# The embedding stage of a four-stage transformer kernel, cut into pipelined rounds, with x1 finished on GpSimd and transposed from its own buffer

## What is computed

```python
# layer 0: adapter with a selected expert, residual, layer norm
hidden = gelu(x @ down_W.T + down_b)
hidden = hidden @ Wsel.T + bsel + domain_emb[idx]
x = hidden @ up_W.T + up_b + x
x = (x - mu) * rsqrt(var + eps) * ln_gamma + ln_beta
# layer 1: adaptive layer norm, projections
x = _ln(x) * (1.0 + scale) + shift          # "x1" of the kernel
q, k, v = x @ Wq + bq, x @ Wk + bk, x @ Wv + bv
# ... attention with a bias of 2 x 16 x 2048 x 2048 and a mask, Wo, feed forward, rotation (layer 2)
# layer 3: U_o, V_o = gram_schmidt(U), gram_schmidt(V), 32 columns of 512 rows each
# basis = U_o @ V_o.T ; the rest of the steering layer
```

## Time and profile before

| | us |
|---|---|
| median of 3 runs | 3924.99 (3924.74 to 3928.07) |
| the profiled execution, its time | 3929.97 |
| its span, first to last instruction | 3927.6 |
| granted PE clock, mean over the span | 0.966 of full |
| PE, DVE, ACT, POOL busy | 3701.7, 2385.5, 2139.4, 2190.1 |

### The profile page before, as it was taken

How to read it: one execution, slowest core, us unless ns; L and a number is a source line. 1 busy time by engine, 2 the same in 40 slices (tenths; PEclk the granted TensorE clock), 3 DMA queues, 4 the chain that set the end, 5 groups by cost and what they waited for, 6 DMA issues and landing times. The chain is left out here.

```text
span 3927.6 us, 80609 instructions
## 1 busy us (share of the span) xinstructions
PE 3701.7 (94%) x32225; PEld 2528.7 (64%) x32225; DVE 2385.5 (61%) x4512; ACT 2139.4 (54%) x2970; POOL 2190.1 (56%) x787
## 2 busy tenths in 40 slices
PE   4888897999999999999999999998799999999997
PEld 2444444888888888888888888887344444444443
DVE  5675673888888888888888888886212111211102
ACT  1222122899998999989999889997111111111110
POOL 2332232999898989989999799996211111111100
PEclk8999898999999999999999999999899999999995
DMA  3334336999999999999999999996300000000005
GB/s 135 114 129 171 129 118 250 359 319 325 321 335 362 325 328 325 328 353 346 323 325 322 358 333 319 327 321 233 149 11 22 33 33 11 22 33 12 11 1 191
DMA packets 209772, 830.94 MB, mean 212 GB/s; under 512 B 23650, under 2 KB 57570, under 8 KB 134148
## 3 DMA queue, kind: packets, MB, share of 16 engines
q1 hardware_dynamic: 205060, 817.53, 60.0%
q10 hardware_dynamic: 4352, 8.39, 0.6%
HBM read 733.04 MB, written 92.80 MB: 210 GB/s over the span
## 5 line engine op out<-in xcount | busy, mean ns | idle before, releaser
L909 POOL TENSOR_TENSOR at_tiles<-at_tiles,at_negmask 128x1792 f32<-128x1792 f32 x512 | 1838.1, 3632 | 241.4 <-DMA at_tiles<-in_bias 204.3
L999 ACT ACTIVATE at_tiles<-at_tiles,at_rmin 128x2048 f32<-128x2048 f32 x512 | 1025.3, 2002 | 78.5 <-DVE at_rmin L1046 78.3
L945 PE MATMUL at_ps_p<-consts,at_tiles 128*128 128x128 f32 x8192 | 1025.6, 272 | 0.1
L945 PEld LDWEIGHTS at_ps_p<-consts,at_tiles 128*128 128x128 f32 x8192 | 931.3, 142 | 36.8 <-ACT at_prob_t L1007 0.6
L1007 ACT ACTIVATE at_prob_t<-at_ps_p 128x512 f32<-128x512 f32 x1536 | 830.2, 596 | 145.4 <-PE at_ps_p L945 145.2
L1046 DVE CUSTOM_DVE_ANT_0 at_tiles<-at_ps_s,at_tiles 128x1024 f32<-128x1024 f32 x512 | 624.7, 1220 | 158.2 <-PE at_ps_s L926 117.5
L926 PE MATMUL at_ps_s<-at_k_stack,at_q_stack 128*128 128x512 f32 x2048 | 680.4, 433 | 37.5 <-DMA at_q_stack<-q_lo 16.7
L1046 DVE CUSTOM_DVE_ANT_0 at_tiles<-at_ps_s,at_tiles,at_rmin 128x1024 f32<-128x1024 f32 x512 | 657.6, 1284 | 18.3
L962 PE MATMUL at_ps_c<-at_prob_t,at_v 128*32 128x128 f32 x16384 | 500.9, 274 | 3.3 <-DMA at_v<-v 1.5
L962 PEld LDWEIGHTS at_ps_c<-at_prob_t,at_v 128*32 128x32 f32 x16384 | 431.7, 110 | 47.0 <-issue 44.6
L1240 PE MATMUL ff_ps_m<-ff_norm_t,ff_w 128*128 128x512 f32 x1024 | 442.2, 592 | 0.8 <-ACT ff_feats L1336 0.8
(11 more groups left out here) (170 smaller groups left out, 2989.0 us busy)
## 6 DMA issues: line engine op xcount, KB each, us to landing
at_tiles<-in_bias SPq DMA_DIRECT2D x512, 1024.0 KB, 9.9
at_k_stack<-k_hi SPq DMA_DIRECT2D x128, 256.0 KB, 7.1
at_k_stack<-k_lo SPq DMA_DIRECT2D x128, 256.0 KB, 9.0
negm<-em_mask_out SPq DMA_DIRECT2D x8, 2048.0 KB, 9.9
at_q_stack<-q_hi SPq DMA_DIRECT2D x128, 128.0 KB, 7.8
at_q_stack<-q_lo SPq DMA_DIRECT2D x128, 128.0 KB, 8.7
at_negmask<-negm SPq DMA_DIRECT2D x32, 512.0 KB, 14.7
at_v<-v SPq DMA_DIRECT2D x64, 256.0 KB, 11.2
```

Of the source, the lines that this page charges most:

```text
L909: pool.tensor_tensor(tiles[:, s, 0:PCOLS], tiles[:, s, 0:PCOLS], negm[:, s, 0:PCOLS], ALU.add).then_inc(s_pool, 1)
L945: last = pe.transpose(ps_p[k][:, y * P:(y + 1) * P], tiles[:, s, t * P:(t + 1) * P], ident)
L999: act.activation(tiles[:, s, :], tiles[:, s, :], ACT.Exp, bias=rmin[:, s, 1:2], scale=-1.0, accum_out=rsum[:, s:s + 1]).then_inc(s_exp, 1)
```

## The change

`embed_stage` is written anew as a pipeline with finer steps; the computation is the same. There are nine rounds r again, each with the front of tile r and the back of tile p = r − 1, but now blocks of the back stand between the steps of the front on PE, and splits between them on DVE.

- PSUM: two banks `ps_t` for transposes, three `ps_q` for the 12 blocks in turn, two `ps_u` for the up product, one `ps_d` for down, expert and the Gram-Schmidt products.
- x1 has a buffer of its own, `x1`, and `x1_t` is double. The x1 transposes of tile r come at the end of round r, two chunks ahead of block 11 and two behind it.
- The first norm is two DVE operations with two tensor inputs: (res − mean) × gamma, then × rstd + beta; POOL's beta is gone. The second norm is applied by ACT (`unit_rows`: res × rstd − mean × rstd), and POOL then multiplies the whole tile, 128x2048, by the scale into `x1` and adds the shift in a second operation of that size.
- A Gram-Schmidt step multiplies on DVE the columns by the current one (264 elements), adds the four chunks up with a `tensor_reduce` to 66 columns, and PE adds over partitions with one matmul against ones. The four steps of a round belong to round r, so they run in rounds 0 to 7; the small products of the end (`gs_end`) are spread over round 8.
- The mask leaves in four pieces of 128x2048 per round through two buffers.

The core of the diff (PE's, ACT's, POOL's and DVE's new order and the new helpers):

```diff
+            def gs_dots(n, k):
+
+                i = STEPS * n + k
+                if k == 0:
+                    pe.wait_ge(s_hid2, n + 1)
+                pe.wait_ge(s_gsr, i + 1)
+                pe.matmul(ps_d[:, 0:2 * (RANK + 1)], ones[:], gs_part[:].rearrange("p m r -> p (m r)"),
+                          start=True, stop=True).then_inc(s_dot, 1)
...
+            x_columns(0, range(DC))
+            for r in range(NT + 1):
+                p, front, back = r - 1, r < NT, r >= 1
+                if front:
+                    down_project(r)
+                if back:
+                    project(p, 0)
+                if front:
+                    expert(r)
+                if back:
+                    project(p, 1)
+                if front:
+                    gs_dots(r, 0)
+                    up_project(r, (0, 1))
+                else:
+                    gs_end(0)
+                    gs_end(1)
+                if back:
+                    project(p, 2)
...
+                    gs_end(4)
+                if back:
+                    project(p, 7)
+                if front:
+                    gs_dots(r, 2)
+                if back:
+                    project(p, 8)
+                if r + 1 < NT:
+                    x_columns(r + 1, (0, 1))
+                if back:
+                    project(p, 9)
+                if r + 1 < NT:
+                    x_columns(r + 1, (2, 3))
+                if front:
+                    gs_dots(r, 3)
+                if back:
+                    project(p, 10)
+                if front:
+                    x1_columns(r, (0, 1))
+                if back:
+                    project(p, 11)
+                if front:
+                    x1_columns(r, (2, 3))
...
+            def unit_rows(n):
+
+                act.wait_ge(s_nmr, n + 1)
+                for j in range(TJ):
+                    act.activation(res[:, j, :], res[:, j, :], ACT.Identity, bias=nmr[:, j:j + 1],
+                                   scale=rstd[:, 1, j:j + 1]).then_inc(s_u, 1)
...
+            def root(n, half):
+                link = Chain(pool, s_plink, 4 + 2 * n + half)
+                pool.wait_ge(s_mv, 2 * n + half + 1)
+                link(pool.tensor_tensor(rstd[:, half, :], mv[:, half, :, 1], eps[:], ALU.add))
+                pool.tensor_tensor(rstd[:, half, :], rstd[:, half, :], minus_half[:], ALU.pow).then_inc(s_rs, 1)
+
+            add_up_bias(0)
+            for r in range(NT):
+                b = batch_of(r)
+                gs_norms(r, 0)
+                root(r, 0)
+                root(r, 1)
+                gs_norms(r, 1)
+                if r + 1 < NT:
+                    add_up_bias(r + 1)
+                gs_norms(r, 2)
+                pool.wait_ge(s_u, 4 * r + 4)
+                after(pool, s_x1_st, 16 * r)
+                if r >= 1:
+                    pool.wait_ge(s_tr, chunk_x1(r - 1, DC - 1) + 1)
+                pool.tensor_tensor(x1[:], res[:], net.ada_scale[:, b, :].unsqueeze(1).broadcast_to([P, TJ, D]),
+                                   ALU.mult).then_inc(s_x1m, 1)
+                gs_norms(r, 3)
+                pool.wait_ge(s_x1m, r + 1)
+                pool.tensor_tensor(x1[:], x1[:], net.ada_shift[:, b, :].unsqueeze(1).broadcast_to([P, TJ, D]),
+                                   ALU.add).then_inc(s_x1, 1)
...
+            def gs_products(src, step):
+                step(v.tensor_tensor(gs_prod[:], src[:], src[:, :, :, 0:1].broadcast_to([P, 2, DC, RANK + 1]), ALU.mult))
+                v.tensor_reduce(gs_part[:], gs_prod[:].rearrange("p m c r -> p m r c"), AX.X, ALU.add).then_inc(s_gsr, 1)
...
+            def gs_project(n, k):
+                i = STEPS * n + k
+                src, to = gs[i % 2], gs[(i + 1) % 2]
+                step = Chain(dve, s_gs, i * 6 + 3)
+                dve.wait_ge(s_nrm, i + 1)
+                step(v.reciprocal(gs_norm[:, 2:4], gs_norm[:, 2:4]))
+                over = gs_norm[:, 2:4].unsqueeze(2)
+                v.tensor_tensor(gs_coef[:], dots[:, :, 1:RANK + 1], over.broadcast_to([P, 2, RANK]),
+                                ALU.mult).then_inc(s_gst, 1)
+                step(v.tensor_tensor(gs_col[:], src[:, :, :, 0], over.broadcast_to([P, 2, DC]), ALU.mult))
+                dve.wait_ge(s_gst, i + 1)
+                step(v.tensor_copy(gsq[:, :, :, i:i + 1], gs_col[:].unsqueeze(3)))
+                step(v.tensor_tensor(gs_proj[:], gs_col[:].unsqueeze(3).broadcast_to([P, 2, DC, RANK]),
+                                     gs_coef[:].unsqueeze(2).broadcast_to([P, 2, DC, RANK]), ALU.mult))
+                step(v.tensor_tensor(to[:, :, :, 0:RANK], src[:, :, :, 1:RANK + 1], gs_proj[:], ALU.subtract))
+                gs_products(to, step)
...
+            def centred(n, j):
+                if j == 0:
+                    dve.wait_ge(s_mv, 2 * n + 1)
+                v.scalar_tensor_tensor(res[:, j, :], res[:, j, :], mv[:, 0, j, 0:1], gamma[:], ALU.subtract,
+                                       ALU.mult).then_inc(s_cen, 1)
+
+            def affine(n, j):
+                if j == 0:
+                    dve.wait_ge(s_rs, 2 * n + 1)
+                dve.wait_ge(s_cen, 4 * n + j + 1)
+                v.scalar_tensor_tensor(res[:, j, :], res[:, j, :], rstd[:, 0, j:j + 1], beta[:], ALU.mult,
+                                       ALU.add).then_inc(s_x0, 1)
+
+            def minus_mean(n):
+                dve.wait_ge(s_rs, 2 * n + 2)
+                v.scalar_tensor_tensor(nmr[:], mv[:, 1, :, 0], -1.0, rstd[:, 1, :], ALU.mult, ALU.mult).then_inc(s_nmr, 1)
...
+                    split(p, 3)
+                if front:
+                    centred(r, 2)
+                    affine(r, 0)
+                    centred(r, 3)
+                    affine(r, 1)
+                    row_stats(r, 1, 0)
+                    affine(r, 2)
+                    row_stats(r, 1, 1)
+                    affine(r, 3)
+                    row_stats(r, 1, 2)
+                    moments(r, 1, row_stats(r, 1, 3))
+                if back:
+                    split(p, 4)
+                if front:
+                    gs_squares(r, 1)
...
+                if front:
+                    minus_mean(r)
+                if back:
+                    split(p, 5)
+                if front:
+                    gs_project(r, 1)
...
+                if back:
+                    split(p, 6)
+                if front:
+                    gs_squares(r, 2)
...
+                if back:
+                    split(p, 7)
+                if front:
+                    gs_project(r, 2)
+                if back:
+                    take_v(p, 0)
+                    take_v(p, 1)
+                if front:
+                    gs_squares(r, 3)
+                if back:
+                    take_v(p, 2)
+                if front:
+                    gs_project(r, 3)
+                if back:
+                    take_v(p, 3)
...
```

557 lines of the change are left out of this document (272 added, 285 removed).

## The result

The changed kernel takes 3869.05 us (median of 4 runs, 3866.31 to 3871.07) against 3926.53 us (3924.74 to 3930.59, 4 runs) for the kernel before on the same chip: 57.5 us less, ratio 0.9852, 95% interval 0.9835 to 0.9869. The prediction was 3871 us in a range of 3832 to 3896.

The account below looks back on a forecast made before the run. PE was taken as busiest, losing time to store waits and the low clock behind them. 101 + 6 × 65.6 + 59.7 + 44 = 598.3 us against 648.87, with 3.5 less behind it, gave 3871 us, range 3832 to 3896.

Parts of the forecast that it names:

- The chain of a round: Steady round followed step by step from the down product through PE, DVE, POOL and ScalarE: 65.6 us.
- The low clock behind the first wait: Block 8, after PE's 6.2 us wait for step 1's products, takes 5.4 instead of 3.4 us; at most 2.0 us loss.
- The lower bound: Steady round if the low clock behind the two PE waits costs nothing: 62.5 us.
- First round: Serial chain of the first tile: down product of round 1 at 101 us against 91.55 today, a loss of 9.5 us.
- The last front round: Round without up bias and x transposes: x1 at 52.9, end at 59.7 us.
- the last round: Round with 12 blocks and the final small products: 44 us.
- pause: Between the embedding stage and attention, waiting for transfers to land: 3.5 us less, bounds 0 and 6.
- 4 × 1.5 = 6 us per round: Gram-Schmidt steps on PE: one 66-column matmul replaces the 16-pass weight loads, a step falling from about 1.7 to 0.2 us.
- Rival A: DVE isn't shut out for whole POOL operations: a round of 61 us, 3839 us in all; chance 0.14.
- Rival B: PE at its floor, waits at both places vanish: 55 us a round, median basis 3798 us; chance 0.04.
- Rival C: Clock stays at 1.2 GHz from first wait to round's end: round about 79 us, 3970 us in all; chance 0.06.
- D: No change: something unseen adds 6 us to a round and the first round loses more, about 3920 us; chance 0.04.

Follow-up runs that it names:

- run 3: Changed kernel with six extra unused matmuls on TensorE ahead of the third small product of rounds 1 to 7: 3868.03 us, ratio 0.9851.
- Runs 6 to 9: On the kernel before: em_res twice, 3873.63 us; one small product per step, 3932.95; both edits, 3885.19; both with each small product issued eight times, 3884.85.
- run 5: Kernel of run 4 with shift straight behind scale, fourth small product inside block 11, and VectorE splitting blocks 6 and 7 later: 3787.85 us, ratio 0.9660.
- run 10: Changed kernel with GpSimd adding the up bias to only two of the next tile's four parts, the rest left zero: 3855.7 us, ratio 0.9822.
- run 1: Changed kernel with GpSimd's up bias of the next tile moved from between the norms of steps 1 and 2 to behind the shift: 3847.91 us, ratio 0.9799.
- run 2: Changed kernel with the up bias at its place but as four operations of 128x512: 3870.3 us, ratio 0.9858.
- run 4: Changed kernel with GpSimd's order scale, norms 2, shift, norms 3, up bias, and TensorE's third and fourth small products later: 3816.13 us, ratio 0.9719.

## Why the prediction was right, and where it was not

**The chain of a round** held nearly step by step. In the round from 299.31 us, predicted and measured: the second aggregates at 32.0 and 31.9; the rows done at 36.8 and 37.0; TensorE at the third small product at 35.6 and 35.8, which it can start at 41.8 and starts at 41.9; the scale from 44.1 to 48.6 in both; the products of step 2 at 50.8 and 50.9; the fourth small product at 52.8 and 53.6; the shift done at 58.8 and 59.6; TensorE's second wait 2.5 and 2.27 us; the round 65.6 and 64.9.

**Terms that were off.** The low clock behind the first wait took 2.6 us in this round (6.21 against 3.60) and up to 2.9 in another, where 2.0 was counted and given as the most it could be. In this round it was paid in block 8 alone: block 11 ran at 3.60 us (in four of six rounds) where 1.5 us more were counted. The reduction takes 0.60 us, not 0.45, and VectorE's affine operations stand 0.66 us apart, not 0.61. These errors nearly cancel, and that is luck: in which rounds block 11 is slow could not be known. The lower bound was added up wrongly, too: without any low clock the sum is 65.6 − 2.0 − 1.5 = 62.1 us a round, not 62.5 (run 3's fast round took 63.0).

**First round**: the down product of tile 1 at 102.8 against a predicted 101. The last front round took 59.0 (59.7), the last round 44.2 (44.0), and the stage ended at 598.9 us (598.3). The **pause** behind it shrank from 20.1 to 14.9 us, 5.2 where I took 3.5; that was within the bounds given. In all the attention stage began 55.3 us earlier, against a predicted sum of 54. The spans differ by 58.7 us and the medians by 57.5; the 3.4 us on top come from code that no edit touched. That 3869 lies within 2 us of 3871 is therefore partly luck; the 54 us are what was right.

**What the change removes** was put wrongly in one point. The saving on TensorE, "4 × 1.5 = 6 us per round", was listed beside the wait for the store as a part of what is gained. Runs 6 to 9, made on the order of the kernel before, show that it is worth nothing there: the end of the store wait alone gives as much as the whole change, and the single small product costs 1.4 us of chain per round and 1.65 us of low clock. In the changed kernel's own order neither was taken out alone, so what each gives there is open. In the kernel of run 5 TensorE has no time left over, and by the same rows 6 us more of its work would lengthen the round; that was not run. The forecast came out because the new round was worked out from its own chain and not from what was removed.

**Rival A** (no lock, rounds of 61 us) is refuted by run 10 and by the 4.12 us rows. Its round length was reached by run 1, which keeps the lock and moves the operation.

**Rival B** (TensorE at its floor) is where the prediction was really wrong. It said that this was "only possible if POOL's work were much shorter; the rows deny it". Run 5 does it with the same three operations of 4.5 us, with GpSimd, TensorE and VectorE in another order, at 53.4 us a round, the floor that the prediction had worked out. The chain that I followed was that of one order, and I took its length for a property of the work. Whether the lock costs anything depends on what VectorE has to deliver behind it.

**Rival C** (the clock stays low to the round's end) did not occur: in four of the six rounds everything behind block 8 ran at the full clock again, in the first and the last block 11 was slow once more (4.71 and 5.29 us), behind the wait for x1. **D** neither.

## What to carry to other kernels

Where two engines hold each other up, cutting the long operation into parts brought nothing (run 2). Place it where nobody waits for what it holds up (run 1), and let two such operations follow each other without small ones between them that need the other engine (run 5, with two more moves). Before an edit is credited with the busy time that it saves, ask which chain closes the round: on the kernel before 6 us less on the busiest engine were worth nothing, 0.35 us more per step on the chain were paid in full, and one more buffer gave the same as a rewritten stage. The rewritten stage went further only when its order was set by the chain. How far the kernel before would go with the second buffer and its up bias in another place was not tried.

## What the runs showed of the hardware that I had not expected

- The low clock behind a wait has no fixed price. Behind 6.09 us of waiting a block took 6.15 to 6.46 us in place of 3.60, and 5.07 in the first of the six rounds; behind 3.93 us 6.30 and 5.35 in turn; behind 2.13 us 5.09 to 5.35 in five rounds and 3.65 in one. The two waits of 1.3 and 1.2 us of run 4 were followed by 5.35 us in three rounds and 3.65 in the next three, with the same work ahead of them. So it can be counted at 0 to 2.9 us a wait, not closer.
- A low clock that is avoided at one wait tends to turn up at the next one: in five of six rounds of run 3, where TensorE was kept busy, and in run 10 by itself. It need not: in the last round of run 3 both blocks were fast.
- GpSimd's four short additions let exactly one VectorE instruction through between two of them (run 2), so that cutting up an operation hardly lessens the sum of the stalls (3.7 us against 4.0).
- It is not only VectorE instructions with two inputs in SBUF that stand still. In run 1 a copy of eight elements, 0.17 us elsewhere, took 4.45 us beside the up bias, and in run 4 a split's first half with one input (L773), 0.42 us elsewhere, took 4.11 beside the scale.
- Stages that no edit touched differ by up to 9 us from kernel to kernel (3253.6 to 3262.9 us), so of a few us only the embedding stage's own rows tell. Why is open.
